# A dynamic convolution on one core: the centre tap of the first pair first, the second weights load gated earlier, and two pieces of pair 1 made by GpSimd

## The reference

```python
def _gn(v, G=32, eps=1e-05):
    g = v.reshape(B_, G, C_ // G, H_, W_)
    m = jnp.mean(g, axis=(2, 3, 4), keepdims=True)
    s = jnp.var(g, axis=(2, 3, 4), keepdims=True)
    return ((g - m) / jnp.sqrt(s + eps)).reshape(v.shape)

pooled = x.mean(axis=(2, 3))                       # x is _gn(x) here
a = relu(einsum('bc,kc->bk', pooled, fc1_w) + fc1_b)
att = softmax(einsum('bk,jk->bj', a, fc2_w) + fc2_b, axis=1)
agg_w = einsum('bk,koihw->boihw', att, weight)     # K = 4 kernels of 64x64x3x3
agg_b = att @ bias
out = x + vmap(conv_one)(_gn(x), agg_w) + agg_b[:, :, None, None]
```

## Time and profile before

| | us |
|---|---|
| median of 3 executions | 304.34 |
| lowest and highest | 304.25, 304.86 |
| the profiled execution | 304.55 |
| its span (first to last instruction) | 302.8 |
| PE busy within the span | 296.9 |
| DVE, ACT, POOL busy | 246.1, 189.6, 17.8 |

### The profile page before, as it was taken

How to read it: one execution, slowest core, us unless ns; L and a number is a source line. 1 busy time by engine, 2 the same in 40 slices (tenths; PEclk the granted TensorE clock), 3 DMA queues, 4 the chain that set the end, 5 groups by cost and what they waited for, 6 DMA issues and landing times.

```text
span 302.8 us, 15876 instructions
## 1 busy us (share of the span) xinstructions
PE 296.9 (98%) x7065; PEld 272.0 (90%) x7065; DVE 246.1 (81%) x799; ACT 189.6 (63%) x246; POOL 17.8 (6%) x30
## 2 busy tenths in 40 slices
PE   7899999999999999999999999999999999999995
PEld 5678997799978997799999999999999889999984
DVE  3898999989999999998998989699696978956000
ACT  3756739194684927385496859577585866768222
POOL 2321040403100000000000000000000000000000
PEclk9999999999999999999999999999999999999999
DMA  7867767737447574846708798865658342332333
GB/s 251 245 222 203 261 212 217 214 133 198 157 144 221 179 210 168 222 155 172 245 19 245 227 248 244 260 176 165 200 133 240 102 122 71 111 102 81 94 114 103
DMA packets 27012, 53.62 MB, mean 177 GB/s; under 512 B 6080, under 2 KB 16704, under 8 KB 26944
## 3 DMA queue, kind: packets, MB, share of 16 engines
q1 hardware_dynamic: 26720, 52.53, 58.9%
q10 hardware_dynamic: 224, 0.07, 0.1%
HBM read 26.89 MB, written 25.69 MB: 174 GB/s over the span
## 4 chain that ended last, share of the span: by engine, by line
PE 94%; DMA 3%; SPq 1%; DVE 1%; ACT 0%; issue 0%; DVEq 0%
PE acc L1068 94%; DMA x<-x 2%; DMA w_sb<-w_t 2%; SPq L316 1%; PE tiny L1005 0%; DVE o L792 0%; ACT wh L864 0%; DVE mix L643 0%; DVE part_mix L638 0%; DVE part_mix L635 0%; DVE rsum L578 0%; DVE rtotal L580 0%; DVEq L790 0%
## 5 line engine op out<-in xcount | busy, mean ns | idle before, releaser
L1068 PE MATMUL acc<-xh,wh 64*64 64x385 f16 (+5 forms) x2304 | 112.4, 325 | 0.1
L1068 PE MATMUL acc<-xh,wl 64*64 64x385 f16 (+5 forms) x2304 | 112.2, 325 | 0.0
L1068 PE MATMUL acc<-xl,wh 64*64 64x385 f16 (+5 forms) x2304 | 111.5, 325 | 0.0
L1068 PEld LDWEIGHTS acc<-xh,wl 64*64 64x64 f16 x2304 | 90.9, 107 | 7.1
L1068 PEld LDWEIGHTS acc<-xl,wh 64*64 64x64 f16 x2304 | 91.7, 107 | 6.2
L1068 PEld LDWEIGHTS acc<-xh,wh 64*64 64x64 f16 x2304 | 90.0, 107 | 7.5 <-ACT wh L864 0.4
L914 ACT ACTIVATE o<-acc,par 128x392 f32<-128x392 f32 (+1 forms) x64 | 42.9, 670 | 56.9 <-PE acc L1068 56.9
L458 DVE BATCH_NORM_STATS2 stats<-x 128x6 f32<-128x448 f32 x105 | 61.3, 619 | 1.9
L835 ACT ACTIVATE xh<-x,xof,xsc 128x1568 f16<-128x1568 f32 x24 | 40.5, 1690 | 25.1 <-DVE xof L545 24.7
L702 DVE TENSOR_TENSOR xl<-x,xh 128x1568 f16<-128x1568 f32 x28 | 49.8, 1784 | 3.3 <-ACT x L802 3.2
L593 DVE SCALAR_TENSOR_TENSOR mix<-w_sb,ex,mix 128x576 f32<-128x576 f32 (+1 forms) x69 | 42.9, 622 | 0.5
(11 more groups left out here) (106 smaller groups left out, 162.1 us busy)
## 6 DMA issues: line engine op xcount, KB each, us to landing
x<-x SPq DMA_DIRECT2D x60, 392.0 KB, 4.2
out<-o SPq DMA_DIRECT2D x36, 196.0 KB, 3.8
out<-o SPq DMA_DIRECT2D x72, 98.0 KB, 2.9
out<-o SPq DMA_DIRECT2D x8, 588.0 KB, 3.7
out<-o SPq DMA_DIRECT2D x16, 294.0 KB, 4.4
w_sb<-w_t SPq DMA_DIRECT2D x2, 576.0 KB, 4.6
x<-x SPq DMA_DIRECT2D x2, 448.0 KB, 4.4
out<-o SPq DMA_DIRECT2D x7, 112.0 KB, 2.2
```

Source lines behind the costliest of these rows:

```text
L1068: ins = nc.tensor.matmul(pixels[:, top:bottom, left:right], weights[i][halves[m], tap * C:(tap + 1) * C], window, start=start and step == ...
```

## The change

Weights: kernels 2 and 3 are asked for when piece 2 of x is in, not piece 4. On PE the mixture of all four kernels is made for the first row of taps: the centre tap in `acc` (64 columns), its two side taps in `tiny` (128 columns); `part_mix` and DVE's addition go. The weights' range comes ahead of the range. ACT makes `wh` from PSUM in four pieces (centre, sides, and the two other rows); PE multiplies the centre tap of groups 0 and 1, then the sides of both, then all three taps of group 2. ACT makes single strips of 392 columns where it made 784; DVE makes strip 6. DVE makes `xl` of pair 0 ahead of pair 1's first statistics. For pair 1 the root is a power on POOL, the sums are put four steps earlier into the stream, one statistics chunk of pair 2 goes behind the logits, and quarter 1 of `xh` is made by POOL and no longer by ACT. Line numbers below are those of the new file's hunks.

```diff
-GATE = 0
+GATES = (0, 2)
-WARM_PRODUCTS = (38, 6, 15, 4, 3, 3)
+WARM_PRODUCTS = (38, 6, 15, 3)
-SUMS_AT = ((1, 2, 6), (1, 2, 2), ...
+SUMS_AT = ((1, 2, 2), (1, 2, 2), ...
...
-            for n, (piece, ks) in enumerate(((GATE, slice(0, 2)), (len(PIECES) - 1, slice(2, K)))):
+            for n, (piece, ks) in enumerate(zip(GATES, (slice(0, 2), slice(2, K)))):
...
@@ gpsimd @@
-            for p in range(EARLY):
+            second_low_inputs(0)
+            pool.wait_ge(s_mv, 2)
+            nc.gpsimd.tensor_tensor(rstd[:], mv[:, 1:2], minus_half[:], ALU.pow).then_inc(s_root, 1)
+
+            pool.wait_ge(s_exp, 2)
+            pool.wait_ge(s_norm, 2)
+            pixels = slice(HALF // 2, HALF)
+            nc.gpsimd.tensor_scalar(xh[1][:, pixels], x_sb[1][:, pixels], xsc[1][:], xof[1][:], ALU.mult,
+                                    ALU.add).then_inc(s_quarter[1], 1)
+            for p in range(1, EARLY):
                 second_low_inputs(p)
@@ vector @@
+            def second_group_stats():
...
+                nc.vector.bn_aggr(mv[:], stats[:].rearrange("p a b -> p (a b)")).then_inc(s_mv, 1)
...
+                dve.wait_ge(s_root, 2)
+                dve.wait_ge(s_fc1, 2)
+                deviation = dict(in0=mv[:, 1:2], scalar=1.0 / WLIMIT, in1=rstd[:], op0=ALU.mult, op1=ALU.mult)
+                stt(out=std[1][:], **deviation).then_inc(s_std, 1)
+                stt(out=sums[:, 0:K], in0=fdiff[:], scalar=rstd[:], in1=b1_part[:], op0=ALU.mult, op1=ALU.add)
...
+                tt(sums[:, RANGE:RANGE + 1], std[1][:], wbound[:], ALU.add).then_inc(s_sums, 1)
...
-                for k in range(SUMMED_SHARES):
+                for k in range(K):
                     nc.vector.tensor_scalar(diagonals[:, k, :], eye[:], ex[:, k:k + 1], None, ALU.mult).then_inc(s_diagonal, 1)
+                for k in range(2):
+                    first_scale_step(k)
+                high_strip(6)
+                low_part(0)
...
-            weights_bound()
-            chunk_stats(1, 0, 1)
             dve.wait_ge(s_scaled, 1)
             low_inputs(0, 0)
+            weights_bound()
+            chunk_stats(1, 0, 1)
             chunk_stats(1, 1, CHUNKS)
             exchange_stats(1)
-            group_stats(1)
+            second_group_stats()
             for p in range(1, EARLY):
                 logits(p)
+                if p == 1:
+                    chunk_stats(2, 0, 1)
                 mixture_in_parts(p)
@@ scalar @@
             first_high(5, 6, s_quarter[2])
-            first_high(2, 4, s_quarter[1])
-            high_weights_part(0, 0)
-            first_high(6, 8, s_quarter[3])
+            first_high(2, 3, s_strip)
+            first_high_weights(0)
+            first_high_weights(1)
+            first_high(3, 4, s_quarter[1])
             first_share(2)
             first_high(0, 1, s_quarter[0])
-            high_weights_part(0, 1)
+            first_high_weights(2)
+            act.wait_ge(s_v_strip, 2)
+            first_high(7, 8, s_quarter[3])
 
             normalise_quarter(0, 1)
-            high_weights_part(0, 2)
+            first_high_weights(3)
...
-                high_quarter(p, 1)
+                if p > 1:
+
+                    high_quarter(p, 1)
@@ tensor @@
+            def centre_share(k):
+
+                pe.wait_ge(s_weights[k // 2], 16)
+                pe.wait_ge(s_diagonal, k + 1)
+                for m in range(2):
+                    nc.tensor.matmul(acc[SLOTS - 1][1][halves[m], CENTRE_SUM], diagonals[halves[m], k, :],
+                                     first_piece(0, w_sb[:, k, :])[halves[m]], start=k == 0, stop=False)
...
+            centre_share(0)
+            sides_share(0)
+            centre_share(1)
+            centre_share(2)
+            centre_share(3)
+            first_residual()
+            for k in range(1, K):
+                sides_share(k)
```

More of the change, by code:

```diff
@@ L863, in high_weights_part, with first_high_weights @@
                 part = PARTS[n]
-                nc.scalar.activation(wh[i][:, part], mix[:, part], ACT.Copy, scale=wsc[i][:]).then_inc(s_wh, 1)
+                nc.scalar.activation(wh[i][:, part], mixed_part(p, n), ACT.Copy, scale=wsc[i][:]).then_inc(s_wh, 1)
+            def first_high_weights(n):
+                if n == 0:
+                    act.wait_ge(s_wsc, 1)
+                    act.wait_ge(s_centre_sum, 2)
+                elif n == 1:
+                    act.wait_ge(s_sides_sum, 2)
+                else:
+                    act.wait_ge(s_part, shares(0, n))
+                nc.scalar.activation(first_piece(n, wh[0]), mixed_piece(n), ACT.Copy, scale=wsc[0][:]).then_inc(s_wh, 1)
             def first_share(n):
@@ L1014, in first_range @@
             def first_range():
+                pe.wait_ge(s_wnorms, 1)
+                nc.tensor.matmul(tiny[1][:, WEIGHTS:WEIGHTS + 1], scale[:], wnorms[:],
+                                 start=True, stop=True).then_inc(s_weights_range, 1)
                 pe.wait_ge(s_first_std, 1)
@@ L1038, in part_sum, with sides_share, first_residual @@
+            def sides_share(k):
+                for m in range(2):
+                    ins = nc.tensor.matmul(tiny[0][halves[m], SIDES_SUM].rearrange("p (t c) -> p t c", c=C),
+                                           diagonals[halves[m], k, :], first_piece(1, w_sb[:, k, :])[halves[m]],
+                                           start=k == 0, stop=k == K - 1)
+                    if k == K - 1:
+                        ins.then_inc(s_sides_sum, 1)
+            def first_residual():
                 pe.wait_ge(s_eye, 1)
```

138 lines of the change are left out of this document (71 added, 67 removed).

## The result

| | before | changed |
|---|---|---|
| median, 15 executions each, same chips, us | 304.80 | 305.45 |
| lowest and highest | 304.19, 305.35 | 304.76, 306.73 |
| the profiled execution | 304.55 | 305.24 |
| its span | 302.8 | 303.4 |

The ratio is 1.0029, with a 95% interval of 1.0020 to 1.0037: the change makes the kernel slower by 0.29%, 0.9 us. The medians differ by 0.65 us and the means by 0.90; the changed kernel has a tail towards long times, and the ratio follows the means more nearly. The lower end of the interval is just the 0.2% that the prediction took as its limit, so the loss is sure, and that it passes the limit is not.

A forecast was written before the change was run, and what follows sets the result against it. PE's product stream bounds the kernel: its start, a fixed amount of products, and any stalls. The profiled 304.55 + 0.15 for the start = 304.70; against the 304.34 median, the forecast is 304.5 us, range 303.9 to 305.7.

The forecast's parts named there:

- rival (a): Pair 1's mixture: POOL's quarter and DVE's shares hinder each other, PE stalls 0.5 to 1.4 us, 305.4; chance 0.28.
- The likeliest case: Whole kernel: start costs 0.15 us, pair 1 nothing; 304.1 to 304.9 us, chance 0.47.
- first share after the wait for `wnorms`: PE's start: one sum, two over `std` and another sum, one idle product less; first share at 12.39 us.
- ninth product, on the path from the first weights: Product stream's start: first product needing the side taps' `wh` starts at 14.59 instead of 14.44, +0.15 us.
- gap ahead of it: PE after the eight centre products: stands 0.33 us, from 14.26 to 14.59, until the side taps' `wh` is ready.
- request for the second weights: Weights load: kernels 2 and 3 asked for about 1.1 us earlier; costed at nothing, otherwise 0 to 0.5 us.
- `mv` after the ninth product: Statistics ahead of pair 1's sums: one more chunk on DVE makes `mv` about 0.6 us later.
- exponential in the stream: Pair 1's inputs on ACT: taken 0.2 us earlier, raising the third `wh` piece's slack from 0.1 to 0.3 us.
- (b): Start at its upper prices, or pair 1's sums late: +0.4 to +0.8, 304.9 to 305.1 us; chance 0.12.
- (c): First weights late by the earlier request: up to 0.5 us on top, 305.0; chance 0.05.
- (d): Start: no wait for the side taps' sum, centre's 0.19 us and more kept, giving 304.0; chance 0.08.
- The lower prices: Start with all step prices at their lower ends: ninth product at 14.27 us, a gain of 0.17.

The follow-up runs named there:

- run 4: Kernel before with kernels 2 and 3 of the weights asked for as early as in the change; 304.61 against 304.63 us, 1.0002.
- run 6: Changed kernel with the first weights asked for one piece of x later; 307.19 against 304.80 us for before, 1.0077.
- run 3: Changed kernel with POOL's quarter waiting only for the scale, not for the exponentials; 304.81 against 304.63 us for before, 1.0013.
- run 2: Changed kernel with quarter 1 of pair 1's `xh` made by ACT again; 304.95 against 304.63 us for before, 1.0011.
- run 5: Kernel before with only quarter 1 of pair 1's `xh` moved to POOL, behind the exponentials; 305.19 against 304.80 us, 1.0012.
- run 1: Changed kernel once more, no edit, a second profile; 305.54 against 304.63 us for before, 1.0026.
- run 10: Changed kernel with 32 idle products for 38 in the first group, twelve instructions fewer on PE; 304.99 us, 1.0024 to before.
- run 8: Changed kernel, quarter not waiting for exponentials, `std` sums ahead of `wnorms` wait, one late idle product for three, centre tap for three groups; 304.49 against 304.80 us, 0.9993.
- run 11: Run 8 with pair 1's sums asked for four products later and 32 idle products for 38; 304.22 against 304.70 us for before, 1.0002.
- run 12: Run 8 with pair 1's sums asked for four products later, idle products kept at 38; 304.56 against 304.65 us for before, 1.0002.

## Why the prediction was wrong where it was

The number fell into the range because the range reached up to rival (a), which is what happened, and because of gaps that the prediction did not have. The likeliest case, no loss in pair 1, was wrong. Of the 0.9 us by the ratio, 0.20 is the start (forecast 0.15), 0.35 is pair 1 (forecast 0), and 0.35 is left for the gaps.

| step | forecast | measured |
|---|---|---|
| first share after the wait for `wnorms` | + 1.10 | + 1.19 (10.77 to 11.96) |
| PE through the shares | 1.53 | 1.51 (11.96 to 13.47) |
| ninth product, on the path from the first weights | + 0.15 | + 0.20 |
| gap ahead of it | 0.33 | 0.33 |
| request for the second weights | 0 | 0 (run 4) |
| `mv` after the ninth product | + 0.6 - 0.15 | + 0.43 |
| sums ready ahead of PE's request | 0.1 | 0.2, no wait |
| exponential in the stream | - 0.2 | - 0.20 |
| POOL's quarter | up to 1.67 | 1.11, 0.99 alone |
| the quarter's cost to PE | 0; by rival (a) 0.5 to 1.4 | 0.35 |
| "issue" gaps | not in it | 0.65 and 0.86 in two traces |

**The start** was right in mechanism and size: a centre piece that comes early is paid back in the wait for the sides. The error of 0.05 us is in the list of sums, 0.09 too low there and 0.02 too high in each of two later steps. The first of the two over `wnorms`, with narrow tiles behind it, takes 0.31 us to the next start (10.77 to 11.08); the second, with full tiles behind it, takes 0.25 (11.29 to 11.54). I had counted 0.24 for each. The pair over `std` took 0.21 where I said 0.20. So both changes of shape seem to cost something, and I had priced one; no run has the same list without them.

**Rivals (b), (c) and (d).** None happened. The prices of the start lay near the values taken. Run 4 left the time where it was, so the earlier request doesn't slow the first weights by anything that shows. But the reason that I gave, room at 154 GB/s, was misread: the same row has a DMA share of 0.82, and in run 6 the core moved 414 GB/s at a share of 1.03. The rate and the share say different things about room. The gap was there as forecast, so the gain of (d) was not.

**The range** doesn't follow from its own terms. The lower prices give 304.34 - 0.17 = 304.17 and not 303.9, and the upper end of (a) is 304.5 + 1.4 = 305.9 and not 305.7. The measured value lies inside either.

**The step that failed is the choice at rival (a).** I had named the overlap, the semaphore that causes it, and the sum for its price, and still put it at 0.28, because short instructions of both engines overlap without harm at the start. That evidence was of another kind: the stretch came only where a long POOL instruction was under way when a DVE instruction with two operands in SBUF began. One with a single such operand was not stretched in that place (the statistics chunk of run 3, 0.63). DVE's `TENSOR_SCALAR` at 27.81, which took its usual 0.32, settles nothing, since it began 0.08 us before POOL's. What the likeliest case put at nothing is the wait of one share for POOL: 0.62 us of delay, of which 0.35 reached PE. Runs 2, 3 and 5 show it from three sides: without the quarter, with the quarter earlier, and with the quarter in before.

The Trainium skill, page "SBUF — State Buffer", section "Who interferes with whom", gives the rule: the second to issue blocks until the first is through. The trace agrees as to who loses: the share began 0.27 us after POOL's instruction and ended at 29.20, behind POOL's end at 29.00. It doesn't show that the share stood still until then, since only 0.20 us of its usual 0.42 came after it, and POOL too took 1.11 us instead of 0.99. By this rule the case should have been the likeliest one.

**The size of (a)** was set too high as well. I took DVE's delay to be POOL's whole duration, 0.8 to 1.67 us. DVE can lose only what is left of it when the share begins, 29.00 - 28.16 = 0.84, and it lost 1.04 - 0.42 = 0.62 of that. The slack that the prediction put at 0.3 measures 0.26 (0.2 from the earlier exponential, 0.06 that before had). Its own formula, delay less slack, with the right delay gives 0.62 - 0.3 = 0.32, and 0.35 is what PE lost.

**What was missing** are the "issue" gaps. They would explain why a loss of 0.20 + 0.35 = 0.55 in the trace is 0.9 us by the ratio. By the length of the stream, less the loss in pair 1, they cost 0.65 us in the changed kernel's trace, 0.86 in run 1, 0.55 in run 3 and 0.06 in run 10. They appear in eight of the nine traces with the new start (not in run 2), and in none of the five with the old one. That is a correlation.

Their places are those of PE's code (run 10), and they lie on a grid: the gaps at 180, 188 and 196 us stand ahead of loads 4,223, 4,351 and 4,608, that is 128 and 257 apart, or about 256 instructions and twice that. The traces also record 55 transfers of 16 KB on an instruction queue, one for 130 of PE's 7,165 loads. The load behind each of the eleven gaps from 50 us on starts 1.3 to 1.6 us after the end of the latest of these transfers. That points to PE waiting for its own code where a piece of it lands late. It is argued from these records and not tested: no run moved such a transfer, and whose code it carries no record says.

The gaps' share of the 0.9 us, some 0.35, is only what is left over; of the 0.65 us between the medians only 0.1 is. The wider spread of the changed kernel (up to 306.7 us, with full clock) is not explained either.

## What to carry to other kernels

Before work is handed to an idle engine, look at what the busy engine starts on the same semaphore: here GpSimd, reading SBUF, and VectorE, with two operands there, were released together, and three quarters of what was left of the long instruction (0.62 of 0.84 us) was charged to the engine on which PE depended. The cure here was to wait for less, not to move the work back. That brought the kernel back to before's time and not below it. A centre piece of the operands made early gains only as many products as it feeds; if the second piece comes later for it, price the second piece first. And compare two traces of a few tenths' difference from the landing of the load that starts them, not from the span's zero, once you have seen that this load does start both.

## What the runs showed of the chip

- A DVE instruction with two SBUF operands took 1.04, 1.03 and 1.03 us (the changed kernel, runs 1 and 5) instead of 0.42 beside a POOL instruction of 1.11 us, which alone took 0.99. Both lose; DVE, the later one, loses more. A statistics instruction of DVE with one operand, begun while POOL's ran, kept its 0.63 us (run 3).
- The first load's data were first used at 8.83 to 9.63 us in eleven traces in which it is asked for behind the same piece of x, and at 10.28 in a twelfth (run 2).
- TensorE's granted clock fell to 0.50 from 15 to 17 us in one execution, after a start in which the sum over `wnorms` came at 12.00 instead of 10.77. The first 36 products took some 3.0 us instead of 1.84, which is 1.1 us and more than any part of this change.
- PE's weight loads stood for 0.2 to 0.9 us at a time with no releaser on record, near 55 us in seven traces (the changed kernel, runs 1, 3, 8, 10, 11 and 12), between 180 and 196 us in four, and not at all in six. The place is fixed by the count of PE's instructions: twelve fewer at the start moved it by six loads and their products.
